# Attention with the value products cut into parts of at most 256 columns, one behind every second step

## What is computed

```python
Q = _apply_rope(proj(W_q)); K = _apply_rope(proj(W_k)); V = proj(W_v)
scores = einsum('bhnd,bhmd->bhnm', Q, K) / sqrt(D_K)
scores = where(tril(ones((S, S))), scores, -inf)
head = einsum('bhnm,bhmd->bhnd', softmax(scores), V)
x = x + einsum('bsi,oi->bso', head, W_o) * silu(ffn(layernorm(x)))
```

## Time and profile before

| | |
|---|---|
| three runs, us | 1016.93, 1017.38, 1026.69; median 1017.38 |
| profiled execution, span from first to last instruction | 1008.0 us |
| what lies around the span (median minus span) | 9.4 us |
| attention, first exponential to last copy | 148.8 to 539.2 us |
| one group in the steady part | 23.83 us |
| busy over the whole span: TensorE, VectorE, ScalarE | 87%, 81%, 72% |
| one exponential of 512 columns, mean in the steady part | 0.61 us |
| granted TensorE clock, mean | 0.931 |

### The profile page before, as it was taken

One profiled execution on the slowest core, in us unless ns is written; L12 is line 12 of the kernel. 1 busy time (PEld: TensorE's weight loads), 2 busy tenths in 40 slices (PEclk: granted clock), 3 DMA queues, 4 the chain that ended last, 5 costly groups with the idle time before them and its releaser, 6 DMA issues. The chain is left out here.

```text
span 1008.0 us, 25094 instructions
## 1 busy us (share of the span) xinstructions
PE 874.2 (87%) x9373; PEld 464.7 (46%) x9374; DVE 816.2 (81%) x1699; ACT 725.7 (72%) x1493; POOL 289.1 (29%) x331
## 2 busy tenths in 40 slices
PE   4999899899999999999898898778999999979960
PEld 3666543334333333333344666533444444458850
DVE  6665499899999999999923766589999999928895
ACT  2666408788888888888784454478999999948851
POOL 4865311111111000000003656500344443005560
PEclk9999859999999999999999888768999999989995
DMA  5579851644445353330004899695354643546637
GB/s 167 223 267 331 280 133 42 205 101 105 110 98 125 89 123 84 68 69 14 13 24 127 277 317 301 226 241 101 67 118 94 114 89 54 136 142 189 206 119 252
DMA packets 121560, 147.20 MB, mean 146 GB/s; under 512 B 19213, under 2 KB 81242, under 8 KB 120800
## 3 DMA queue, kind: packets, MB, share of 16 engines
q1 hardware_dynamic: 116064, 133.74, 48.0%
q0 software_dynamic: 5376, 11.85, 4.1%
HBM read 77.63 MB, written 69.54 MB: 146 GB/s over the span
## 5 line engine op out<-in xcount | busy, mean ns | idle before, releaser
L854 ACT ACTIVATE probsB<-psB 128x512 f32<-128x512 f32 (+2 forms) x640 | 310.0, 566 | 87.1 <-PE psB L928 61.5
L766 DVE TENSOR_REDUCE mxB<-psB 128x1 f32<-128x512 f32 (+2 forms) x448 | 256.9, 642 | 11.1 <-PE psB L892 8.3
L921 PE MATMUL psB<-q_groups,k_groups 64*128 64x512 bf16 (+3 forms) x768 | 205.8, 330 | 16.6 <-DVE mxB L766 8.3
L892 PE MATMUL psB<-k_groups,q_groups 64*128 64x512 bf16 (+3 forms) x768 | 217.0, 344 | 2.8 <-PEq L293 1.7
L959 PE MATMUL psB<-probsB,vB 128*32 128x512 f32 (+3 forms) x1536 | 164.5, 500 | 0.7 <-ACT probsB L854 0.5
L1725 ACT ACTIVATE psD<-psD 128x896 f32<-128x896 f32 (+2 forms) x192 | 153.4, 799 | 12.9 <-PE psD L1779 12.7
L921 PEld LDWEIGHTS psB<-q_groups,k_groups 64*128 64x128 bf16 x768 | 67.5, 94 | 161.2 <-ACT probsB L854 140.3
L1656 DVE TENSOR_REDUCE sumsD<-psD 128x1 f32<-128x128 f32 (+3 forms) x256 | 113.2, 481 | 11.8 <-PE psD L1802 9.4
L899 PE MATMUL psB<-hideB,chooseB 64*128 64x128 bf16 (+1 forms) x1024 | 115.1, 210 | 0.0
L1779 PE MATMUL psD<-k_groups,q_groups 64*128 64x512 bf16 (+3 forms) x384 | 104.4, 343 | 12.3 <-ACT psD L1725 5.6
L766 DVE TENSOR_REDUCE mx2B<-psB 128x1 f32<-128x384 f32 (+2 forms) x192 | 104.4, 594 | 8.5 <-PE psB L899 6.9
(11 more groups left out here) (227 smaller groups left out, 1504.5 us busy)
## 6 DMA issues: line engine op xcount, KB each, us to landing
v<-vaugA SPq DMA_DIRECT2D x4, 2048.0 KB, 8.9
vB<-v SPq DMA_DIRECT2D x16, 512.0 KB
q_groups<-q SPq DMA_DIRECT2D x32, 200.0 KB
k_groups<-k SPq DMA_DIRECT2D x32, 200.0 KB
q_groups<-q SPq DMA_DIRECT2D x32, 192.0 KB
k_groups<-k SPq DMA_DIRECT2D x32, 192.0 KB
back<-emptyB POOLq DMA_DIRECT2D x16, 256.0 KB, 3.8
o<-outB SPq DMA_DIRECT2D x128, 32.0 KB, 1.8
```

Of the source, the lines that this page charges most:

```text
L766: nc.vector.tensor_reduce(dst, src, AX.X, ALU.max).then_inc(max_read, 1)
L854: nc.scalar.activation(probs[:, n % DEEP, 0:w], st[n % BANKS][:, 0:w], ACT.Exp, scale=DH ** -0.5).then_inc(exp_done, 1)
L892: ins = nc.tensor.matmul(bank[:, to:to + w], q[half[r], s, hq // 2, t * P:t * P + P], k[half[r], s, hq // 2, HALF * c:HALF * c + w], start ...
L921: ins = nc.tensor.matmul(bank[:, to:to + w], k[half[r], s, hq // 2, jt * P:jt * P + P], q[half[r], s, hq // 2, i0:i0 + w], start=True, sto ...
```

## The change

`products` now takes a part of a slot. Slots of 512 and 384 columns are cut into two parts (256 and 192 columns each), slots of 256 and 128 stay whole, which makes 20 parts in place of 12 products. The waits stand ahead of the first part and `pv_done` rises with the last. The parts are issued behind every odd step: slot 0 behind steps 7 and 9, slot 1 behind 11 and 13, slot 2 behind 15, slot 3 behind 17, slot 4 behind 19 and 21, slot 5 behind 23 and 25, slot 6 behind 27 and 29, slot 7 behind 31 and 33, slot 8 behind 35 and 37, slot 9 behind 39, and in the next group slot 10 behind step 1 and slot 11 behind 3 and 5. The copy of the first half moves from behind the exponential of step 16 to that of step 17 (`HALF_AT`), the copy of the second half from step 4 to step 5 (`END_AT`).

```diff
@@ -611,7 +611,17 @@
     last_step = [max(n for n, (j, _) in enumerate(steps) if j == jj) for jj in range(SLOTS_B)]
     AHEAD, DELAY = 16, 4
     RING, BANKS = 4, 3
-    LAG, DEEP = 5, 16
+    LAG, DEEP, PART = 4, 16, HALF // 2
+
+    chunks = [(j, i, -(-slot_width(j) // PART)) for j in range(SLOTS_B) for i in range(-(-slot_width(j) // PART))]
+    issue_at, free = [], 1
+    for j, _, _ in chunks:
+        at = max(free, last_step[j] + LAG)
+        issue_at.append(at)
+        free = at + 2
+    assert all(at % 2 for at in issue_at) and issue_at[0] + UNITS >= free
+    HALF_AT = max(at for at, (j, _, _) in zip(issue_at, chunks) if j == 3)
+    END_AT = issue_at[-1] - UNITS
 
     def stream(x):
 
@@ -853,9 +863,9 @@
                         act.wait_ge(st_done, n + 1)
                         nc.scalar.activation(probs[:, n % DEEP, 0:w], st[n % BANKS][:, 0:w], ACT.Exp,
                                              scale=DH ** -0.5).then_inc(exp_done, 1)
-                        if e == last_step[3] + LAG:
+                        if e == HALF_AT:
                             keep(x, 0)
-                        if e == LAG - 1 and x:
+                        if e == END_AT and x:
                             keep(x - 1, 1)
                         if x == NQ - 1 and e == TURN_AT + 2:
                             for part, half_of in enumerate(halves):
@@ -943,27 +953,27 @@
                                 if causal:
                                     causal(i, part)
 
-                def products(x, j):
+                def products(x, j, i, parts_of):
 
                     c, jt = slots[j]
                     s = x % QUADS
                     w = slot_width(j)
-                    pe.wait_ge(exp_done, UNITS * x + last_step[j] + 1)
-                    if x < GROUPS_AHEAD and j == 0:
-                        pe.wait_ge(in_loaded[s], LOADS)
-                    if jt == 0 and x + c:
-                        pe.wait_ge(out_kept, 2 * x + c)
+                    part = w // parts_of
+                    if i == 0:
+                        pe.wait_ge(exp_done, UNITS * x + last_step[j] + 1)
+                        if x < GROUPS_AHEAD and j == 0:
+                            pe.wait_ge(in_loaded[s], LOADS)
+                        if jt == 0 and x + c:
+                            pe.wait_ge(out_kept, 2 * x + c)
                     for hq in range(4):
                         at, heads = next((e, heads) for e, (jj, heads) in enumerate(steps) if jj == j and hq in heads)
-                        to = offset(heads, hq, w)
-                        ins = nc.tensor.matmul(pv[VW * hq:VW * hq + VW, HALF - w:HALF], v[:, s, jt, VW * hq:VW * hq + VW],
-                                               probs[:, (UNITS * x + at) % DEEP, to:to + w], start=(jt == 0),
+                        to = offset(heads, hq, w) + part * i
+                        col = HALF - w + part * i
+                        ins = nc.tensor.matmul(pv[VW * hq:VW * hq + VW, col:col + part], v[:, s, jt, VW * hq:VW * hq + VW],
+                                               probs[:, (UNITS * x + at) % DEEP, to:to + part], start=(jt == 0 and i == 0),
                                                stop=(j in (3, SLOTS_B - 1)), skip_group_check=True)
-                    ins.then_inc(pv_done, 1)
-
-                def due(x, j):
-                    at = last_step[j] + LAG
-                    return UNITS * x + (at - 1 if at < UNITS and slot_width(steps[at][0]) == P else at)
+                    if i == parts_of - 1:
+                        ins.then_inc(pv_done, 1)
 
                 def output_projection():
                     pe.wait_ge(g2["const"], 16 * 7)
@@ -989,7 +999,7 @@
                         turn_over(x)
                     else:
                         side_by_side(for_maximum(x, g))
-                waiting = []
+                due = [(UNITS * x + at, (x, *chunk)) for x in range(NQ) for at, chunk in zip(issue_at, chunks)]
                 for x in range(NQ):
                     todo = stream(x)
                     pe.wait_ge(neg_placed[x % 2], PLACED * (x // 2 + 1))
@@ -1000,17 +1010,15 @@
                         if todo:
                             both.append(for_maximum(*todo.pop(0)))
                         side_by_side(*both)
-                        if e == last_step[j]:
-                            waiting.append((x, j))
-                        if waiting and due(*waiting[0]) <= UNITS * x + e:
-                            products(*waiting.pop(0))
+                        if due[0][0] == UNITS * x + e:
+                            products(*due.pop(0)[1])
                         if x == NQ - 1 and e == PROJECT_AT:
                             output_projection()
                         if x == NQ - 1 and e == TURN_AT:
                             turn_rows()
                     assert not todo
-                for y in waiting:
-                    products(*y)
+                for _, chunk in due:
+                    products(*chunk)
```

## The result

The changed kernel takes 1024.97 us (median of 20 runs, 1022.17 to 1034.83) against 1017.58 us before (20 runs on the same chips). The ratio is 1.0077, 95% interval 1.0053 to 1.0100: 7.4 us slower, and inside the 1% within which the forecast put it.

A forecast was written before the change was run, and what follows sets the result against it. TensorE was taken to bind at 23.5 us a group, with 0.85 of copy waits 24.35 against 23.83; thirteen groups gave +6.8, the ends +0.8, together +7.6 on 1017.4: 1025.0 us, range 1012 to 1033.

The forecast's parts named there:

- TensorE becomes the bound, 23.5 us of work: Per steady group, TensorE's work rises from 21.6 to 23.5 us, over VectorE's 22.61.
- A cut costs 0.15 + 0.10: On TensorE, each cut adds 0.15 us fixed per product and 0.10 ahead of it, 0.25 us together.
- The copies cost 0.85 us per group: TensorE waits for bank 7's copies: second half 0.2 to 0.3 us, first half 0.57 to 0.64.
- A group of 24.35: Steady group takes 23.5 + 0.85 us, 0.52 more than 23.83; thirteen groups give +6.8 us.
- The gap behind step 28 goes: VectorE's 0.62 us wait for scores behind the reduction of step 28 should vanish.
- The ends, +0.8 us: First group adds nothing; group 14's cuts and clock give +0.8 us, between -1.5 and +3.
- The faster ones: VectorE stays the bound as fixed costs hide, 1001.5 us, chance 0.04; or copies do not decide, 1013 to 1014, chance 0.2.
- The one that feared waits for exponentials: With three banks, steps wait for the exponential three steps earlier: group 25.0 us, 1032 to 1034; chance 0.26 over 1027.5.

The follow-up runs named there:

- cuts in place: All eight slots cut, but both parts kept together where the whole product stood in the kernel before, copies unmoved; 1020.74 us, ratio 1.0034.
- even bursts: Against the kernel before, parts cut at multiples of 128 columns and gathered into 12 bursts of 256 to 512 columns per group; 1019.58 us, ratio 1.0026.
- whole products at the new places: No slot cut, each whole product and both copies moved to the changed kernel's places; 1038.56 us, ratio 1.0179 to the kernel before.
- copies spaced: Changed kernel with slot 3 moved to step 15, slot 11's parts together behind step 3, copies behind 16 and 4; 1025.38 us.
- joined versions: Kernel before with slot 6 cut and slots 9, 10 together, 1016.73 us; slots 2, 3 too, 1012.89; or slots 0, 6 cut and 2, 3 together, 1009.25.

## Why the prediction was right

- *TensorE becomes the bound, 23.5 us of work.* Right. The parts have the lengths taken (0.57 to the next step), and the group less its two waits for copies is 23.44.
- *A cut costs 0.15 + 0.10.* The sum of 0.25 held for a part that stands alone, and that is what the change makes. But the split was wrong: I laid the 0.15 to the eight added instructions, and in the cuts in place and the even bursts these cost 0.01. All 0.25 is the price of one change from scores to value products and back. So the rule that a change of the tiling mode drains TensorE, which I had cited for the 0.10 (the Trainium skill, TensorEngine Tiling, "Key Properties"), fits the whole 0.25, though no run here tells a drain from another cost of the same change. The rule that weight loads can be pulled ahead of running matmuls (the Trainium skill, TensorE: Matmul & The Clock Gate, "Architectural detail"), against which I had held the idle loads, agrees with the trace within a burst: eight more loads there cost 0.01 us. The load behind the burst in the earlier trace rows did not run ahead.
- *The copies cost 0.85 us per group.* The waits measured are 0.26 and 0.60, where 0.2 to 0.3 and 0.57 to 0.64 were worked out. Taking the copies' work away gave less, 0.57 us, because 0.18 of the waits stayed and 0.14 came anew ahead of the transpose. The kernel before already paid 0.25 for its copies.
- *A group of 24.35.* Measured 24.30, and term by term: 23.44 for 23.5, and 0.86 for 0.85. Thirteen of them gave +5.9 in place of +6.8 us.
- *The gap behind step 28 goes.* Right: part and steps follow each other there at 0.30 and 0.57.
- *The ends, +0.8 us.* The whole attention gained 6.5, so they gave 0.6. The clock did not hold. The wait in group 14 shrank from 2.94 to 2.08 us and the granted clock still went to the lower level, as the timeline of TensorE and a window (columns as in the earlier trace rows) show:

```profile
507.35 0.27 PE L884 MATMUL psB<-identC,partsB 128*64 128x128 f32 x1 [2.08 <-POOL partsB L831]
508.04 1.08 PE L972 MATMUL psB<-probsB,vB 128*32 128x256 f32 x8
```

```profile
508.00:509.00 1.00, 1.00 (x10) 0.20 (x8) 1.00 (x2) 0.82 (x2) 0.00 (x0) 0.50 0.00 0
```

- *The rivals.* The faster ones fell, because each of the 20 parts stands alone and pays its switch. The one that feared waits for exponentials fell for the changed kernel, whose parts behind every second step cover them. It came true in other versions that leave steps without a burst: in the whole products at the new places, the copies spaced and the even bursts steps wait 0.31 to 0.59 us for exponentials, and in the joined versions too. Four steps without a burst are not enough for it. Steps 17 to 20 of the kernel before are such a stretch, and the wait there is put down to VectorE's reductions (7.7 us in 13 times).

The forecast of 1025.0 met the median of 1024.97 closer than its steps deserve, and that closeness is luck: the groups gave 0.9 us less than forecast and the medians moved by 0.9 more than attention did. The mechanism and its terms are not luck.

## What to carry to other kernels

Count an engine's work by the distances between starts before loading it further: TensorE had 2.2 us of slack in 23.83 here, and a change that fixed a gap of 0.62 us on VectorE spent 2.0 us of TensorE on it. Cut only the one instruction that stands in the way, and keep parts together where nothing has to run between them, since what costs is the change between two kinds of products. When a result buffer is handed over between engines, leave between the end of one use and the start of the next as many steps as the copy and the work queued ahead of it need, and take away the copying engine's work, not only the place of the wait, to learn what the wait is worth.

## What was not expected of the hardware

- Cutting fp32 matmuls to half their columns cost almost nothing while they stood together: 16 instructions of 256 columns took 1.01 us to the next step, eight of 512 took 1.00, and 24 of three slots 1.01.
- Behind a wait of 2.08 us on TensorE in group 14 the granted clock fell from 1.00 (506 to 507 us) to 0.50 (508 to 509 us), and a part of 256 columns took 1.08 us there in place of 0.64.
